# Attention and a routed expert layer on one core: result rows scattered home, batched expert numbers, latent attention a step earlier, scores in 32-row groups

## The chip, the cores and the metric

One core of one Trainium2 chip runs the whole kernel. The metric is the device time of one execution in microseconds (us), median of several runs. Everything is fp32 unless said otherwise.

## What is computed

The input x has 4 x 1024 tokens of 256 channels, 4096 tokens in 32 blocks of 128. The reference adds two branches of the layer to x; cut to what matters here:

```python
# branch 1, attention: local attention of 16 heads of 16 channels over the 128 tokens before,
# latent attention of 4 heads over means of 16 tokens, mixed by a sigmoid gate, then out_w
scores = einsum('bhnqd,bhnkd->bhnqk', qb, kb) * scale        # 32 blocks, 16 heads
attn = softmax(where(allowed, scores, NEG)); out = einsum('bhnqk,bhnkd->bhnqd', attn, vb)
lattn = softmax(einsum('bhsd,bhld->bhsl', rq, rk) * lscale)   # latent
mixed = gate * local + (1 - gate) * remote
# branch 2, experts: 64 experts (256 -> 128 -> 256), each token goes to 8 of them
tidx, tw = _gate(x, gate_w, gate_bias)
for e in experts: acc += w_dense[:, e] * ((silu(x @ wg) * (x @ wu)) @ wdn)
# and one shared expert of the same form
```

## The kernel before, in words

The five engines run hand-written streams, with semaphores between them; there is no planner. The stages follow one another in time.

**Setup** (to about 113 us): normalise x, route every token, give each of its 8 copies a slot in a table that is sorted by expert and padded to tiles of 128 rows (`slot8`, `slot_idx`), and write for each tile the number of its expert (`expert_row`, `pair_row`).

**First attention half**, `attention(0)`, blocks 0 to 15. Each engine has a `body` of eight steps `s`, one for each of eight pairs of heads. TensorE (PE): `scores(i, p)` (L833, two matmuls of 128 rows of q against 192 keys for a pair, in one of two PSUM banks `psS`), `turn_probs` (L847, transposes of the probabilities of two steps before), `values` (L859 to L861) and, spread over the steps, the projections, the shared expert and the latent attention: `latent_scores` in step 4 (L867), `latent_turn` and `latent_values` both in step 7 (L873, L879), `latent_out_turn` in step 0 of the next block (L885). The q operand `qz` is q multiplied by `own_head`, a mask of 8 columns, so that each head's 128-row column block is zero but for its own 16 rows: `keep_q` (L1480) writes 1024 values a partition, twice a block. VectorE (DVE): `mask_pair` (L1535 to L1537: mask, row maximum), `mix_sums`, `mix`, `latent_max` in step 5. ScalarE (ACT): `exps` (L1126), `keep_prT` (L1134), `latent_exp` in step 6, `keep_lprT` in step 7. Meanwhile GpSimd (POOL) scatters the normalised tokens into `slot_rows` with 256 indirect DMAs (L599), paced by waits on TensorE's progress.

**Experts**: 160 pairs of tiles. SyncE (SP) loads a pair (`load_pair`, L433, `xs`), TensorE transposes it (L944), runs gate and up (L960), and down (L969); ScalarE copies the two experts' weights from a ring of eight to `wt` (`keep_weights`, L1231 to L1236: for each tile it reads the expert's number from `expert_row` with `value_load`, L1233), applies silu (L1226) and copies the transposed tokens (`keep_tiles`, L1220); VectorE multiplies (L1614), copies the result out (`keep_y`, L1621), and for the first 128 pairs computes two routing weights (L1439). SP stores the pair to `slot_outs` (L437). POOL loads the next experts' weights into the ring (L567 to L569). The order on ScalarE in one step for pair u is `keep_weights(u+1)`, `silu(u)`, `keep_tiles(u+1)`; gate and up of pair u+1 waits for all of its copies.

**Second attention half**, `attention(HALF)`, blocks 16 to 31, with the same bodies. POOL gathers the 8 result rows of each token from `slot_outs` (256 indirect DMAs, L658, paced by TensorE's progress), and VectorE adds them, weighted, to `x_all` (`combine`, L1588). SP stores finished blocks.

## Time and profile before

| what | us |
|---|---|
| runs, median of 3 | 1552.17 (1544.11 to 1554.71) |
| the profiled execution, by its own clock | 1566.45 |
| span of its trace, first to last instruction | 1564.9 |

The profiled execution is 14.3 us (0.9%) above the median. A profile's rows are times of that one execution. An engine's "busy" is the union of its instructions; "idle before" is what lay ahead of a group's instructions, with what ended it; names ending in q are an engine's sequencer, which reads registers, waits on semaphores and issues DMAs. PE is TensorE's matmuls, PEld its weight loads.

### The profile page before, as it was taken

What the parts mean: (1) busy time and instruction counts of PE and PEld (TensorE: products, weight loads), DVE (VectorE), ACT (ScalarE), POOL (GpSimd) and SP (SyncE); (2) the same over time, 40 slices, a digit from 0 to 9 for tenths busy, and PEclk for the clock granted to TensorE, in tenths of its full rate; (3) what the DMA queues carried; (4) which work ended last, traced back from release to release, by engine and by line L of the source; (5) the groups of instructions that cost most, each with busy time, mean ns of one, the idle gap of its engine ahead of it and who ended that gap; (6) DMA issues with size and microseconds to landing.
All of it is one profiled execution on the core that took longest, in us unless ns stands there. A gap on an engine that the chain in (4) does not pass through costs nothing.

```text
span 1564.9 us, 38388 instructions
## 1 busy us (share of the span) xinstructions
PE 1349.8 (86%) x9265; PEld 1227.1 (78%) x9267; DVE 847.4 (54%) x3412; ACT 912.1 (58%) x2383; POOL 721.9 (46%) x868
## 2 busy tenths in 40 slices
PE   3946878789889889999999999999779798887986
PEld 3936777678788779898889898989678687776876
DVE  6763444444445434444444444433456777667777
ACT  2314556565555566666666666666445565555654
POOL 7525666666666602223222223100566666666662
PEclk9767989988988989999999999999988989899988
DMA  7134443342222216767777767655233223232331
GB/s 224 48 152 168 138 151 134 127 158 84 91 87 91 87 45 193 214 211 222 220 214 213 220 203 223 201 161 158 85 88 86 86 80 91 80 87 84 89 87 50
DMA packets 151276, 212.47 MB, mean 136 GB/s; under 512 B 20929, under 2 KB 126146, under 8 KB 150210
## 3 DMA queue, kind: packets, MB, share of 16 engines
q1 hardware_dynamic: 117442, 114.41, 23.5%
q0 software_dynamic: 33792, 97.56, 19.7%
q8 instruction: 19, 0.31, 0.1%
q14 instruction: 23, 0.19, 0.0%
HBM read 111.24 MB, written 100.66 MB: 135 GB/s over the span
## 4 chain that ended last, share of the span: by engine, by line
PE 76%; issue 7%; DVE 6%; another core or an unknown queue 5%; ACT 3%; SPq 2%; DVEq 0%; DMA 0%; ACTq 0%
PE psS L960 19%; PE psS L833 10%; PE psT L847 5%; PE psT L944 5%; PE psO L969 4%; PE psM L969 4%; PE psQ L780 3%; PE psV L820 2%; PE psV L791 2%; PE psT L861 2%; PE psQ L801 2%; PE psT L860 2%; PE psT L859 1%; PE psO L861 1%
## 5 line engine op out<-in xcount | busy, mean ns | idle before, releaser
L658 POOL DMA_INDIRECT shared_mem<-slot_outs,idx_st x256 | 275.3, 1075 | 153.2 <-issue 79.2
L960 PEld LDWEIGHTS psS<-sm,wt 128*128 128x128 f32 x2560 | 299.5, 193 | 40.7 <-ACT sm L1220 37.4
L599 POOL DMA_INDIRECT slot_rows<-x_out_st,idx_st x256 | 259.2, 1013 | 156.4 <-issue 58.4
L960 PE MATMUL psS<-sm,wt 128*128 128x128 f32 x2560 | 325.8, 281 | 3.3 <-ACT sm L1220 1.3
L833 PE MATMUL psS<-kT,qz 128*128 128x192 f32 x1024 | 248.0, 367 | 22.6 <-issue 11.9
L1235 ACT COPY wt<-shared_mem 128x512 f32 x320 | 197.9, 618 | 101.7 <-issue 99.3
L1134 ACT COPY prT<-psT 128x384 f32<-128x384 f32 x256 | 121.9, 476 | 222.5 <-remote 144.3
L1126 ACT ACTIVATE pr<-sm,nmax 128x192 f32<-128x192 f32 x512 | 205.1, 449 | 35.9 <-issue 17.1
L847 PE MATMUL psT<-ident,pr 128*128 128x128 f32 x768 | 141.3, 297 | 71.1 <-ACT prT L1134 56.5
L833 PEld LDWEIGHTS psS<-kT,qz 128*128 128x128 f32 x1024 | 181.3, 209 | 23.8 <-issue 19.3
L567 POOL DMA_DIRECT2D shared_mem<-in_L_ffn_We_gate x56 | 39.4, 704 | 334.4 <-PE psM L969 181.7
L1537 DVE CUSTOM_DVE_ANT_0 sm<-psS,pr 128x192 f32<-128x192 f32 x512 | 162.1, 354 | 51.9 <-issue 49.6
L847 PEld LDWEIGHTS psT<-ident,pr 128*128 128x128 f32 x768 | 100.4, 153 | 107.4 <-issue 99.9
L1614 DVE TENSOR_TENSOR prT<-psS,prT 128x256 f32<-128x256 f32 x160 | 68.0, 425 | 204.1 <-ACT prT L1226 204.1
L1588 DVE SCALAR_TENSOR_TENSOR x_all<-shared_mem,w,x_all (+1 forms) x256 | 123.9, 484 | 0.8
L1535 DVE MEMSET met<- 1x1 f32 x256 | 15.1, 59 | 198.8 <-PE psS L833 139.9
L1220 ACT COPY sm<-psT 128x512 f32<-128x512 f32 x160 | 93.7, 586 | 15.6 <-PE psT L944 9.3
L944 PE MATMUL psT<-ident,pr 128*128 128x128 f32 x640 | 97.5, 276 | 3.9 <-issue 2.3
L1226 ACT ACTIVATE prT<-psS 128x256 f32<-128x256 f32 x160 | 61.3, 383 | 54.2 <-PE psS L960 53.5
L1480 DVE TENSOR_TENSOR qz<-qT,own_head 128x1024 f32<-128x1024 f32 x64 | 78.3, 1223 | 10.9 <-ACT qT L1060 10.1
L969 PE MATMUL psO<-shared_mem,prT 128*128 x320 | 82.5, 381 | 0.2 <-DVE prT L1614 0.2
L969 PE MATMUL psM<-shared_mem,prT 128*128 x320 | 82.4, 380 | 0.0
(266 smaller groups left out, 2465.6 us busy)
## 6 DMA issues: line engine op xcount, KB each, us to landing
pr<-slot_rows SPq DMA_DIRECT2D x160, 256.0 KB, 3.1
slot_outs<-sm SPq DMA_DIRECT2D x160, 256.0 KB, 2.4
slot_rows<-wt SPq DMA_DIRECT2D x16, 512.0 KB
shared_mem<-in_L_ffn_We_gate POOLq DMA_DIRECT2D x56, 128.0 KB, 3.6
shared_mem<-in_L_ffn_We_up POOLq DMA_DIRECT2D x56, 128.0 KB, 3.8
shared_mem<-in_L_ffn_We_down POOLq DMA_DIRECT2D x56, 128.0 KB, 3.8
x_all<-in_L_attn_x SPq DMA_DIRECT2D x4, 1024.0 KB, 9.7
xn_tiles<-sm SPq DMA_DIRECT2D x32, 128.0 KB, 1.7
```

The lines of the kernel that those rows point to most:

```text
L599: pool.indirect_dma_start(slot_rows, bass.IndirectOffsetOnAxis(ap=idx_st[:, j, k:k + 1], axis=0), x_out_st[:, j % 2, :], None).then_inc(sc ...
L658: pool.indirect_dma_start(rows_in[:, j, k, :], None, slot_outs, bass.IndirectOffsetOnAxis(ap=idx_st[:, j, k:k + 1], axis=0)).then_inc(rows ...
L833: last = mm(psS[:, p % 2, u * WIN:(u + 1) * WIN], qz[:, c, u, heads, :].rearrange("p h t -> p (h t)"), kT[:, c, u * UQ:u * UQ + WIN], star ...
L847: last = nc.tensor.transpose(psT[:, 0, a * P:(a + 1) * P], flat[:, a * P:(a + 1) * P], ident[:])
L944: last = nc.tensor.transpose(psT[:, j % 2, (a * DC + c) * P:(a * DC + c + 1) * P], xs[:, j, a, c * P:(c + 1) * P], ident[:])
L960: last = mm(psS[:, j % 2, (2 * a + n) * P:(2 * a + n + 1) * P], wt[j % 2][:, a, c, n * F:(n + 1) * F], xsT[:, j % 2, a, c, :], start=(c == ...
L969: last = mm((psM, psO)[j % 2][:, a * D:(a + 1) * D], hT[:, j % 2, a, :], ring_d[:, e % RING, :], start=True, stop=True)
L1126: nc.scalar.activation(pr[:, p % 4, par, :], sm[:, p % 4, par, :], ACT.Exp, bias=nmax[:, p % 4, par:par + 1], scale=-1.0).then_inc(probs, 1)
L1134: nc.scalar.copy(prT[:, p % 2].rearrange("p a t -> p (a t)"), psT[:, 0, 0:3 * P]).then_inc(prT_ready, 1)
L1235: last = nc.scalar.copy(wt[j % 2][:, a, :, :], ring_gu[:, e % RING, :, :])
L1537: v.tensor_tensor_reduce(sm[:, p % 4, u, :], psS[:, p % 2, u * WIN:(u + 1) * WIN], mask[:, u * WIN:(u + 1) * WIN], -1.0, -FLOOR, ALU.add, ...
L1588: ins = v.scalar_tensor_tensor(x_all[:, t, :], row, w8[:, t, k:k + 1], x_all[:, t, :], ALU.mult, ALU.add)
```

## The change

- **Rows home.** A row of `slot_rows` grows from 256 to 272 words: the token's 8 slot numbers and the (negative, shifted) number of its first home row follow it. In the expert stage VectorE works out from them, for each row of a pair, which of the token's 8 places it is (`keep_meta`, five small instructions and self-waits), and POOL writes the pair's result rows to their home in `home_rows` with two indirect DMAs (`send_home`); padding rows go to spare rows. In the second half SP loads the 8 rows of a block's tokens with one plain DMA of 1 MB; POOL has nothing to do there. The expert weights' loads move from POOL to SP, the pair loads from SP to ScalarE, and the result buffers go from two to four. The stage's first pair loads wait on ScalarE for what SP waited for.
- **Expert numbers.** ScalarE reads `pair_row` (both numbers in one word) for four pairs at once, ahead of each group of four steps.
- **Latent attention.** Scores in step 3, maximum in 4, exponential in 5, transposes and their copy in 6, values in 7.
- **Scores.** `qz` is kept for two heads a 32-row group (mask `own_half`, 256 values a partition), and `scores` runs on even steps only, for two pairs at once: matmuls of 32 rows, the two pairs' in turn, in neighbouring row groups and different banks. VectorE masks both pairs in that step.

```diff
-XS, YS = 4, 2
+XS, YS = 4, 4
+ROW = 272
+META = K + 1
+HOME = T * K + 2 * YS * P
...
+            def send_home(j, u):
+                pool.wait_ge(y_kept, u + 1)
+                pool.sem_inc(blocks_begun, 1)
+                for a in range(2):
+                    pool.indirect_dma_start(home_rows, bass.IndirectOffsetOnAxis(ap=row_idx[:, j, a:a + 1], axis=0),
+                                            ys[j][:, a, :], None).then_inc(y_out[j], 16)
+
+            with pool.Fori(0, PAIRS // YS) as g:
+                for j in range(YS):
+                    send_home(j, g * YS + j)
...
+            def load_rows(j, t):
+                sp.dma_start(rows_in[:, j, :, :], home[t]).then_inc(rows_ready[j], 16)
...
-                    pe.wait_ge(masked, 2 * (n - 1))
-                heads = slice(p % PPC * 2, p % PPC * 2 + 2)
+                    pe.wait_ge(masked, 2 * n)
                 for u in range(2):
-                    last = mm(psS[:, p % 2, u * WIN:(u + 1) * WIN], qz[:, c, u, heads, :].rearrange("p h t -> p (h t)"),
-                              kT[:, c, u * UQ:u * UQ + WIN], start=True, stop=True)
-                last.then_inc(s_ready, 1)
+                    for m in (p, p + 1):
+                        r = slice(m % PPC * 2 * HD, (m % PPC + 1) * 2 * HD)
+                        last = mm(psS[:, m % 2, u * WIN:(u + 1) * WIN], qz[r, c, u, :, :].rearrange("p h t -> p (h t)"),
+                                  kT[r, c, u * UQ:u * UQ + WIN], start=True, stop=True)
+                        if u == 1:
+                            last.then_inc(s_ready, 1)
...
-                    if live:
+                    if live and s % 2 == 0:
                         scores(i, s, nth)
...
+                    if s == 6 and live:
+                        latent_turn(i)
                     if s == 7 and live:
-                        latent_turn(i)
+                        latent_values(i)
...
-                    if s == 4 and live:
+                    if s == 3 and live:
                         latent_scores(i, nth)
...
+            def experts_of(u):
+                word = act.value_load(pair_row[0:1, bass.ds(u, 1)], min_val=0, max_val=E * E - 1)
+                return word % E, word // E
+
-            def keep_weights(j, u, first):
+            def keep_weights(j, u, experts, first):
                 if not first:
                     act.wait_ge(gu_ready, u - 1)
-                for a in range(2):
-                    e = act.value_load(expert_row[0:1, bass.ds(2 * u + a, 1)], min_val=0, max_val=E - 1)
+                for a, e in enumerate(experts):
                     act.wait_ge(experts_ready, e + 1)
...
+            def load_pair(j, u):
+                act.dma_start(xs[j], slot_pairs[u]).then_inc(xs_in[j], 16)
+
...
+                if ahead and nth > 0:
+                    act.wait_ge(row_meta, u)
+                    load_pair((j + XS - 1) % XS, u + XS - 1)
...
                 with act.Fori(1, PAIRS // XS - 1) as g:
+                    named = [experts_of(g * XS + j + 1) for j in range(XS)]
                     for j in range(XS):
-                        step(j, g, MANY, False)
+                        step(j, g, MANY, False, named)
...
-                v.tensor_tensor(qz[:, c, :, :, :], bcast(qT[:, c, :].rearrange("p (u t) -> p u t", u=2), HPC, 2),
-                                bcast(bcast(own_head[:], UQ, 2), 2, 1), ALU.mult).then_inc(q_kept, 1)
+                v.tensor_tensor(qz[:, c, :, :, :], bcast(qT[:, c, :].rearrange("p (u t) -> p u t", u=2), 2, 2),
+                                bcast(bcast(own_half[:], UQ, 2), 2, 1), ALU.mult).then_inc(q_kept, 1)
...
+            def keep_meta(j, u, turn):
...
+                for a in range(2):
+                    last = v.scalar_tensor_tensor(nth_parts[:, a, :], xs[j][:, a, D:D + K], own_slot[:, j % 2, a:a + 1], nth_slot[:],
+                                                  ALU.is_equal, ALU.mult, accum_out=row_nth[:, a:a + 1])
+                last.then_inc(row_steps, 1)
+                v.tensor_scalar(own_slot[:, (j + 1) % 2, :], own_slot[:, j % 2, :], 2.0 * P, None, ALU.add)
+                dve.wait_ge(row_steps, 2 * u + 1)
+                v.tensor_tensor(nth_parts[:, :, 0], xs[j][:, :, D + K], row_nth[:], ALU.add).then_inc(row_steps, 1)
+                dve.wait_ge(row_steps, 2 * u + 2)
+                v.scalar_tensor_tensor(row_idx[:, j, :], nth_parts[:, :, 0], float(HOME), row_at[:, j, :], ALU.add, ALU.min).then_inc(row_meta, 1)
```

Also: the clearing of unused slots is cut into 32 DMAs instead of 16, each block staged for the scatter takes one more DMA of 9 words a row, and POOL prepares some 15 small constants in the setup.

## Rows read from the trace of the kernel before

**Rows 1.** Windows: the three stages. Time, busy time by engine, TensorE clock, DMA.
```profile
core 0: us, PE busy (x) PEld busy (x) DVE busy (x) ACT busy (x) POOL busy (x), PEclk, DMA share, GB/s
113.70:560.00 446.30, 369.85 (x2391) 340.67 (x2392) 209.38 (x981) 256.19 (x813) 269.47 (x288) 0.89 0.34 120
600.00:1098.00 498.00, 493.02 (x3691) 446.72 (x3690) 223.53 (x816) 337.26 (x613) 107.49 (x165) 1.00 0.67 204
1105.00:1552.00 447.00, 377.55 (x2456) 342.55 (x2456) 307.82 (x1243) 264.63 (x840) 281.62 (x287) 0.90 0.29 84
```

**Rows 2.** The chain that ended last, by engine and by line, whole span.
```profile
PE 76%; issue 7%; DVE 6%; another core or an unknown queue 5%; ACT 3%; SPq 2%; DVEq 0%; DMA 0%; ACTq 0%
PE psS L960 19%; PE psS L833 10%; PE psT L847 5%; PE psT L944 5%; PE psO L969 4%; PE psM L969 4%; PE psQ L780 3%; PE psV L820 2%; PE psV L791 2%; PE psT L861 2%; PE psQ L801 2%; PE psT L860 2%; PE psT L859 1%; PE psO L861 1%
```

**Rows 3.** Timeline of TensorE in a block of the second half: one scores group.
```profile
1528.19 0.90 PE L833 MATMUL psS<-kT,qz 128*128 128x192 f32 x4
1528.92 0.49 PE L847 MATMUL psT<-ident,pr 128*128 128x128 f32 x3
```

**Rows 4.** Groups of instructions, attention: line, engine, tiles, count, busy, mean ns, idle before.
```profile
L833 PE MATMUL psS<-kT,qz 128*128 128x192 f32 x1024 | 248.0, 367 | 22.6 <-issue 11.9 <-DVE qz L1480 9.6
L833 PEld LDWEIGHTS psS<-kT,qz 128*128 128x128 f32 x1024 | 181.3, 209 | 23.8 <-issue 19.3 <-DVE qz L1480 2.0
L879 PE MATMUL psM<-rv,lprT 128*128 (+1 forms) x128 | 24.9, 327 | 20.0 <-ACT lprT L1144 15.1 <-issue 4.8
L885 PE MATMUL psM<-ident,lat 128*128 128x128 f32 x32 | 12.3, 383 | 25.2 <-issue 20.7 <-DVE lat L1515 4.3
L847 PE MATMUL psT<-ident,pr 128*128 128x128 f32 x768 | 141.3, 297 | 71.1 <-ACT prT L1134 56.5 <-issue 13.6
L1480 DVE TENSOR_TENSOR qz<-qT,own_head 128x1024 f32<-128x1024 f32 x64 | 78.3, 1223 | 10.9 <-ACT qT L1060 10.1 <-issue 0.4
L1467 DVE TENSOR_TENSOR dif<-small,remote_z 128x256 f32<-128x256 f32 x32 | 13.4, 420 | 0.0
```

**Rows 5.** Groups of POOL: the gathers and the scatters.
```profile
L658 POOL DMA_INDIRECT shared_mem<-slot_outs,idx_st x256 | 275.3, 1075 | 153.2 <-issue 79.2 <-remote 33.7 <-PE psO L861 20.5
L599 POOL DMA_INDIRECT slot_rows<-x_out_st,idx_st x256 | 259.2, 1013 | 156.4 <-issue 58.4 <-remote 33.5 <-PE psO L861 24.5
```

**Rows 6.** Timeline of ScalarE in the expert stage.
```profile
613.12 0.58 ACT L1220 COPY sm<-psT 128x512 f32<-128x512 f32 x1
613.96 0.62 ACT L1235 COPY wt<-shared_mem 128x512 f32 x1 [0.26 <-issue]
614.80 0.62 ACT L1235 COPY wt<-shared_mem 128x512 f32 x1 [0.22 <-issue]
615.84 0.38 ACT L1226 ACTIVATE prT<-psS 128x256 f32<-128x256 f32 x1 [0.42 <-PE psS L960]
...
619.44 0.58 ACT L1220 COPY sm<-psT 128x512 f32<-128x512 f32 x1
620.60 0.62 ACT L1235 COPY wt<-shared_mem 128x512 f32 x1 [0.57 <-issue]
```

**Rows 7.** Sequencers in the expert stage: ScalarE's lookups, TensorE's, SP's loads.
```profile
L1233 ACTq FUSED_REGOPS  x613: 57/152/157, 590.7 to 1089.6; - x154
L1233 ACTq TENSOR_LOAD <-expert_row x309: 271/278/987, 590.4 to 1089.3; - x155
L1233 ACTq SEQ_ASSERT  x309: 18/18/18, 590.9 to 1089.8; - x155
...
L949 PEldq TENSOR_LOAD <-pair_row x2: 307/310/314, 607.3 to 608.0; - x2
...
L433 SPq DMA_DIRECT2D pr<-slot_rows x154: 377/378/848, 592.8 to 1088.6; - x154
DMA to landing us min/median/max: 2.6/3.1/4.6
```

**Rows 8.** Groups of VectorE and ScalarE, expert stage.
```profile
L1439 DVE SCALAR_TENSOR_TENSOR small<-shared_mem,slot 128x64 f32 x254 | 61.2, 279 | 0.0
L1621 DVE COPY sm<-psO 128x512 f32<-128x512 f32 x77 | 53.3, 692 | 43.5 <-PE psO L969 43.5
L1614 DVE TENSOR_TENSOR prT<-psS,prT 128x256 f32<-128x256 f32 x154 | 65.4, 425 | 188.3 <-ACT prT L1226 188.3
L1515 DVE TENSOR_TENSOR lat<-psM,lrec 128x64 f32<-128x64 f32 x32 | 7.2, 225 | 1.3 <-issue 0.2
```

More of the change, by code:

```diff
@@ new lines, in announce @@
+            def announce(j, g):
+                sp.wait_ge(weights_in[j], 48 * (g + 1))
+                sp.sem_inc(experts_ready, 1)
+            for j in range(2):
+                load_expert(j, RING + j)
+            with sp.Fori(1, (E - RING) // 2) as g:
+                for j in range(2):
+                    announce(j, g - 1)
+                    load_expert(j, RING + 2 * g + j)
+            for j in range(2):
+                announce(j, (E - RING) // 2 - 1)
+            sp.wait_ge(pairs_done, PAIRS + 1)
@@ new lines, in _ @@
+            for j in range(ROWS):
+                load_rows(j, j)
+            for j in range(ROWS):
+                announce_rows(j, 0)
+            with sp.Fori(1, NB // ROWS) as g:
+                for j in range(ROWS):
+                    sp.wait_ge(combined, (g - 1) * ROWS + j + 1)
+                    load_rows(j, g * ROWS + j)
+                    store_block((g - 1) * ROWS + j)
+                    announce_rows(j, g)
+            for j in range(ROWS):
+                store_block(NB - ROWS + j)
@@ L1261, in _ @@
             act.wait_ge(cleared, 16 * (E // ZROWS))
+            for j in range(2):
+                act.wait_ge(scattered[j], 16 * K * (NB // 2))
             experts()
@@ L1625, in step @@
                 make_h(j, u, nth < 2)
+                keep_meta(j, u, g)
                 if nth > 0:
-                    keep_y((j - 1) % XS, u - 1, 2 * g + (j + 1) // YS - 1, nth <= 2)
+                    keep_y((j - 1) % XS, u - 1, g if j > 0 else g - 1)
             def experts():
```

222 lines of the change are left out of this document (95 added, 127 removed).

## Prediction, made before the changed kernel ran

> **What bounds the kernel now.** I read the windows first, stage by stage, since an average over the span would mix three different limits [rows 1]. In the expert stage TensorE is busy 493.0 of 498.0 us at full clock: nothing but TensorE counts there, 160 pairs take some 3.16 us each, and no other engine may come between two pairs. The two attention halves take 446 and 447 us for about 15.7 blocks each, some 28.3 us a block, with TensorE busy 83% and 84% at a granted clock of 0.89 and 0.90; the rest is waiting. Setup and seams make up what is left. The chain of waits says the same from the other side [rows 2]: 76% TensorE, with scores 10% of 1564.9, 156 us. The groups then tell what TensorE waits for in attention [rows 4], and ScalarE's timeline how little room it has in the expert stage [rows 6].
>
> **Scores in row groups.** A pair's scores, four passes, hold TensorE from 1528.19 to 1528.92, 0.73 us, 0.18 a pass at full clock [rows 3]; 256 pairs are 187 us at that rate, 156 on the chain. Now two pairs go together, eight passes in the order g g h h g g h h over two row groups. If a pass can run beside a neighbour in the other group, but not beside one in its own, eight slots become five: 0.91 instead of 1.46 us, 0.55 less for each of 128 double pairs, 70 us. Against this, each double pair stands between full-height matmuls, so the array changes its shape twice; what a change costs no row shows. Today's weight loads run under the matmul before (181 us busy beside 248, only 23.8 idle ahead [rows 4]); without that cover one load, 0.209 on average, is bare. I take 0.15 for each of 256 changes, 38 us. Net -32. Bounds: -93 if the passes halve and a change is free, +38 if nothing overlaps and only the changes are paid.
>
> The Trainium skill ("TensorEngine Tiling (Array Packing)", Key Properties) says that changing the tiling mode, and not merely the tile, drains TensorE, and this speaks against placing the groups singly among full-height work. By its silence on a price the sum can't be made; with a drain of one pass, 0.18, at all 256 changes it would be 46 instead of 38 us. No row of this kernel shows such a change. The Trainium skill ("TensorE: Matmul & The Clock Gate", Measured speedup vs the span model) gives 3.07 times for four tiles of 32 rows; by an estimate from that page, two tiles would save about half of the 187 us, the same as the lower bound, and no row here shows it.
>
> **Latent attention a step earlier.** TensorE idles 20.0 us before the latent values, since their transposes stand just ahead and ScalarE must copy between, and 25.2 us before the turn of the result [rows 4]. A step of other work now lies between each. Of these 45 us I take 30; the rest ends on "issue", which need not be this. Bounds -45 and 0: if steps 4 and 5 of VectorE are fuller, someone else waits the little that is left.
>
> **keep_q.** 64 instructions of 1.22 us become about 0.42 each, the price of a 256-wide one [rows 4]: 51 us less on VectorE. TensorE waits on it only 9.6 us [rows 4], and VectorE is busy 47% of the first half and 69% of the second [rows 1], so it is mostly cover. I take -10; bounds -51 and 0.
>
> **Order of the scores.** The even pair's distances stay as they are; the odd pair's scores come a step earlier, so its transposes find their probabilities ready. TensorE idles 71.1 us before the transposes [rows 4]. Half of the pairs gain: -20, bounds -57 and +10 (both banks are now waited for together).
>
> **Second half without gathers.** 256 gathers, 275 us of POOL [rows 5], were paced so as to wait for TensorE, never the reverse; DMA was at 0.29 [rows 1]. VectorE's 8 additions a block stay. -5; bounds -30 (VectorE waits less for a late row) and +15 (a 1 MB load at once beside the stores).
>
> **Expert stage, ScalarE.** This is the term that costs. Sequencer and engine go in lock step here: a copy starts when the sequencer has gone through the lookup before it. After the tile copy starts (613.12) the first weight copy starts 0.84 later, the second again 0.84 later, silu, waiting for gate and up, at 2.72, after only 0.42 of idling [rows 6]. One lookup is a load of 0.278, register work of 0.06 and 0.15, an assertion of 0.018 and the gaps between, 0.60 in all [rows 7]. Now the sequencer, after a tile copy has started, does: the wait and the issue of the pair load, 0.378 on SP [rows 7], with its registers 0.55; at a group's head the loop's branch, 0.3 (1.16 from tile to weight copy there, against 0.84 [rows 6]); four lookups in a row, 2.40; addresses, 0.2. That is 3.45 until the first weight copy, then 0.65 and 0.62, and silu at 4.72 instead of 2.72: 2.0 us late. Silu of pair u+1 stands ahead of the tile copy of pair u+2, for which gate and up waits, and TensorE has no slack to give back, so each group of four pairs is 2.0 us longer: 38 loop heads and the shorter last one, 77 us. The three other pairs of a group lose nothing: 0.55 + 0.2 until the first copy, no lookup, 2.05 till the end of the second, before 2.72. Bounds: 0 if the four lookups overlap in the sequencer, of which TensorE's two in a row (0.31 each, started 0.7 apart [rows 7]) show no sign; +88 if nothing at all is hidden.
>
> **Expert stage, the rest.** VectorE has for each pair 0.43, 0.69 and two routing weights of 0.36 less an overlap, about 1.6 [rows 8]; keep_meta adds five small instructions, 0.2 to 0.28 each by the nearest ones [rows 8], with waits about 1.5. 3.1 of 3.16: hidden, the more so under the longer groups, but with nothing left; bounds 0 and +30 (0.2 on 128 pairs). POOL has two scatters, 2.6 to 2.8 us with gaps by the 1.013 and 1.075 of the halves [rows 5]: hidden. DMA moves the same rows at 0.67 share [rows 1]: 6% more on loads, hidden.
>
> **Seams.** The first pair loads start after ScalarE has finished attention, and four lookups stand ahead of the second pair: +3. The last rows go home by POOL, and q waits for them: +3. Bounds +2 and +12. Setup constants and the longer scatter rows lie beside VectorE's and TensorE's work: 0, at most +5.
>
> **Sum.** -32 - 30 - 10 - 20 - 5 + 77 + 0 + 6 = -14, against the profiled execution's 1566.45; the same difference on the median of 1552.17 gives 1538.
>
> **Rivals.**
> *The lookups are cheap.* If the four reads overlap, or their time falls under other waits, the 77 becomes 0 to 15 and everything else stands: -91 to -76, and with VectorE's part about 1470. For it: an edit that only cuts the count of lookups from 8 to 4 a group and leaves their total shorter. Against it: rows 6 and 7. Chance 0.27.
> *Slower: row groups without overlap.* If passes in neighbouring groups go one after another and each change of shape is paid, scores are +38 instead of -32 and the expert stage still loses 77: +56, 1608. It decides from the point at which a double pair takes more than 1.46 us. For it: no row here shows a 32-row pass. With half of that effect the kernel is at 1573. Chance 0.30.
> *VectorE becomes the bound of the expert stage.* keep_meta of over 1.6 us makes every pair late, whatever ScalarE does: +30 beside the cheap lookups, about 1500 in all, or hidden beside the dear ones. Chance 0.08.
> My forecast has 0.35.
>
> **How the numbers follow.** Time 1538, own range 1505 to 1570. For 8 in 10 the range reaches from 1455 to 1605. A difference under 1% can't be told from none in this kernel's runs. Faster by over 1% (below 1536.6): 0.27 and 0.07 from the first and third rivals, 0.17 of the forecast, 0.51. Within 1% (to 1567.7), which is about what a measurement of this kernel can tell from no change: 0.14 of the forecast, 0.05 of the second rival's upper part, 0.01: 0.20. Slower: 0.29.
>
> **What would show it.** Right: the expert stage at 580 to 600 us with TensorE near 87%, ScalarE's chain interrupted by 2 us once in four pairs, blocks of 25 us in attention, scores groups of about 1.2 us for two pairs, no idling before the latent values. Wrong: pairs still 3.16 us apart throughout (the lookups); scores groups of 1.5 us or more (no overlap); pairs evenly 3.4 us apart (VectorE); blocks that stay at 28 us although scores are shorter (then the bound in attention was not TensorE).

## The result, and the profile after

The changed kernel takes 1615.14 us (median of 3 runs, 1611.31 to 1615.46) against 1552.17: a ratio of 1.041, 95% interval 1.035 to 1.048. It is slower by 63 us; 1538 was forecast, with 1570 as the end of the narrow range and 1605 of the wide one. The profiled execution took 1615.46 us with a span of 1613.7, 48.8 us longer than the span of before; that is less than 63 because the profiled execution of before lay 14.3 us above its median.

For what follows one plain fact about the runs is needed: the kernel before itself was met at two levels, 1355 us beside e1 to e4 and e13 to e16, and 1552 to 1564 us in the first measurement and beside all other runs, so every ratio below is between kernels that ran side by side on one chip, and "the 1355 level" and "the 1560 level" name the two.

The windows of the three stages after the change, in the columns of [rows 1]:

```profile
106.00:560.00 454.00, 362.01 (x2397) 310.92 (x2397) 180.44 (x980) 252.15 (x811) 255.88 (x289) 0.83 0.36 128
590.00:1235.00 645.00, 536.96 (x3792) 479.34 (x3790) 320.43 (x1931) 319.61 (x631) 300.15 (x314) 0.97 0.55 165
1243.00:1600.00 357.00, 327.67 (x2448) 282.24 (x2448) 281.68 (x1241) 260.17 (x838) 1.66 (x2) 0.96 0.31 106
```

Three different things happened. The first half is where it was, with TensorE waiting more and at a lower granted clock (0.83, was 0.89). The expert stage, almost pure TensorE before and 517 us from its first to its last gate-and-up matmul, takes 650, with the engine busy 83% of the window above. The second half is 90 us shorter, and POOL has next to nothing to do in it (1.66 us). Laid end to end between the same marks of the two traces (VectorE's copy of the first and of the last block's mask in each half, first gate-and-up matmul of the first and of the last pair; the last column is after minus before):

| stretch | before | after | difference |
|---|---|---|---|
| start to the first mask | 113.7 | 105.9 | -7.8 |
| first half, 15 blocks | 432.3 | 436.0 | +3.7 |
| seam into the experts | 33.4 | 42.8 | +9.4 |
| experts | 516.9 | 650.3 | +133.4 |
| seam out | 8.5 | 7.8 | -0.7 |
| second half, 15 blocks | 421.5 | 330.5 | -91.0 |
| last mask to the end | 38.6 | 40.4 | +1.8 |

The first row is no gain of the change: e7 and e18, one and the same kernel, reach their first mask at 115.7 and 109.4 us.

The groups of the page (columns as in [rows 4]), whole span:

```profile
L956 PE MATMUL psS<-sm,wt 128*128 128x128 f32 x2560 | 341.9, 289 | 106.6 <-ACT sm L1216 88.9
L828 PE MATMUL psS<-kT,qz 32*128 32x192 f32 x1024 | 125.3, 362 | 12.3 <-DVE qz L1493 6.8
L843 PE MATMUL psT<-ident,pr 128*128 128x128 f32 x768 | 146.6, 303 | 48.7 <-ACT prT L1130 25.7
L666 POOL DMA_INDIRECT home_rows<-sm,row_idx x160 | 153.3, 958 | 195.1 <-DVE sm L1635 156.5
```

Scores are busy 125.3 us instead of 248.0 [rows 4] at an unchanged mean of 0.36 us for one (362 and 367 ns), so neighbouring row groups do overlap. TensorE's wait before the probabilities' transposes fell from 71.1 to 48.7 us. In the same view without the page's cut the latent values wait

```profile
L875 PE MATMUL psM<-rv,lprT 128*128 (+1 forms) x128 | 19.0, 275 | 0.8 <-issue 0.8
L881 PE MATMUL psM<-ident,lat 128*128 128x128 f32 x32 | 11.7, 365 | 14.7 <-DVE lat L1528 9.0 <-issue 5.7
```

0.8 us instead of 20.0, and the turn of the result 14.7 instead of 25.2. Every wait that the attention part aimed at became smaller, and the first half did not get shorter. In the expert stage gate and up now wait 106.6 us, 88.9 of them for ScalarE's copy of the turned rows. ScalarE's timeline at the head of a group of four pairs (to be read beside [rows 6]):

```profile
798.56 0.59 ACT L1216 COPY sm<-psT 128x512 f32<-128x512 f32 x1
798.72 0.38 ACTq L1238 DMA_DIRECT2D pr<-slot_rows  x1
802.64 1.14 ACT L1234 COPY wt<-shared_mem 128x512 f32 x2 [3.49 <-issue]
803.24 0.39 ACTq L1238 DMA_DIRECT2D more_mem<-slot_rows  x1
803.68 0.37 ACT L1222 ACTIVATE prT<-psS 128x256 f32<-128x256 f32 x1
803.96 0.57 ACT L1216 COPY sm<-psT 128x512 f32<-128x512 f32 x1
```

From the tile copy's start to the first weight copy's are 4.08 us at this head, and the engine idles 3.49 of them on "issue": its sequencer goes through a pair load, the branch and four lookups. Over the 39 heads of this trace the median is 3.58 until the weight copy and 4.66 until silu; the prediction had 3.45 and 4.72.

### The profile page after: what moved, and what is told of

Same layout as the page of the kernel before. It is cut to its first block, busy times and chain, and to the rows that moved or that the text cites. A ratio compares the mean times of both kernels' runs of the same rounds, so it can differ in the third digit from the quotient of the medians.

```text
span 1613.7 us, 38398 instructions
## 1 busy us (share of the span) xinstructions
PE 1316.8 (82%) x9266; PEld 1151.7 (71%) x9267; DVE 891.0 (55%) x4532; ACT 876.8 (54%) x2383; POOL 630.0 (39%) x749
## 4 chain that ended last, share of the span: by engine, by line
PE 43%; DVE 15%; issue 14%; ACTq 9%; ACT 8%; another core or an unknown queue 8%; DVEq 1%; DMA 1%; SPq 0%
PE psS L956 14%; ACTq L1226 4%; PE psS L828 4%; PE psT L843 3%; DVE x_all L1602 3%; ACTq L1238 2%; PE psV L814 2%; PE psV L785 2%; PE psT L940 2%; DVE sm L1550 2%; ACT pr L1122 2%; ACT sm L1216 2%; PE psM L965 2%; PE psQ L774 2%
## 5 line engine op out<-in xcount | busy, mean ns | idle before, releaser
L956 PE MATMUL psS<-sm,wt 128*128 128x128 f32 x2560 | 341.9, 289 | 106.6 <-ACT sm L1216 88.9
L956 PEld LDWEIGHTS psS<-sm,wt 128*128 128x128 f32 x2560 | 313.6, 200 | 153.2 <-ACT sm L1216 117.2
L639 POOL DMA_INDIRECT slot_rows<-x_out_st,idx_st x256 | 248.2, 970 | 170.4 <-issue 54.5
L1234 ACT COPY wt<-shared_mem 128x512 f32 x320 | 182.7, 619 | 140.3 <-issue 71.7
L666 POOL DMA_INDIRECT home_rows<-sm,row_idx x160 | 153.3, 958 | 195.1 <-DVE sm L1635 156.5
L666 POOL DMA_INDIRECT home_rows<-more_mem,row_idx x160 | 153.6, 960 | 194.1 <-DVE more_mem L1635 144.5
L843 PE MATMUL psT<-ident,pr 128*128 128x128 f32 x768 | 146.6, 303 | 48.7 <-ACT prT L1130 25.7
L1550 DVE CUSTOM_DVE_ANT_0 sm<-psS,pr 128x192 f32<-128x192 f32 x512 | 153.6, 354 | 36.6 <-issue 29.8
L828 PE MATMUL psS<-kT,qz 32*128 32x192 f32 x1024 | 125.3, 362 | 12.3 <-DVE qz L1493 6.8
L828 PEld LDWEIGHTS psS<-kT,qz 32*128 32x128 f32 x1024 | 84.9, 193 | 36.9 <-issue 30.1
L940 PE MATMUL psT<-ident,pr 128*128 128x128 f32 x480 | 76.7, 285 | 5.0 <-issue 4.0
L774 PE MATMUL psQ<-xTs,wqk 128*128 128x128 f32 x512 | 73.4, 303 | 0.5 <-ACT xTs L1066 0.5
```

Of the source, the lines that this page charges most:

```text
L639: pool.indirect_dma_start(slot_rows, bass.IndirectOffsetOnAxis(ap=idx_st[:, j, k:k + 1], axis=0), x_out_st[:, j % 2, :], None).then_inc(sc ...
L666: pool.indirect_dma_start(home_rows, bass.IndirectOffsetOnAxis(ap=row_idx[:, j, a:a + 1], axis=0), ys[j][:, a, :], None).then_inc(y_out[j] ...
L828: last = mm(psS[:, m % 2, u * WIN:(u + 1) * WIN], qz[r, c, u, :, :].rearrange("p h t -> p (h t)"), kT[r, c, u * UQ:u * UQ + WIN], start=Tr ...
L843: last = nc.tensor.transpose(psT[:, 0, a * P:(a + 1) * P], flat[:, a * P:(a + 1) * P], ident[:])
L956: last = mm(psS[:, j % 2, (2 * a + n) * P:(2 * a + n + 1) * P], wt[j % 2][:, a, c, n * F:(n + 1) * F], xsT[:, j % 2, a, c, :], start=(c == ...
L1234: last = nc.scalar.copy(wt[j % 2][:, a, :, :], ring_gu[:, e % RING, :, :])
```

## The experiments

### First set: lookups, way home, gathers, scores

e1 puts the lookup back in front of each pair (and drops the reads at a group's head):

```diff
-                    keep_weights((j + 1) % XS, u + 1, named[j], nth == 0)
+                    keep_weights((j + 1) % XS, u + 1, experts_of(u + 1), nth == 0)
```

Expected: 

> The changed kernel with the four-pair lookups undone: one read of pair_row ahead of each pair's weight copies. Theory L (the batch of four lookups, 2.4 us in one go, is what the expert stage lost): the long gaps once in four pairs vanish, the stage falls from 645 to about 515 us, 1615 to about 1490. Theory G (GpSimd's indirect DMAs hold up TensorE's signals to the other engines, and the lookups are only one part of the loss): 77 us at most go, 1535 to 1560, and pairs of 4 to 5 us remain, scattered. Rival: a lookup in every pair is itself exposed behind the DMA issue, 0.1 to 0.4 us a pair, and only 20 to 60 us go.

e2 sends the result rows with plain DMAs, so they don't go to their own places:

```diff
-                    pool.indirect_dma_start(home_rows, bass.IndirectOffsetOnAxis(ap=row_idx[:, j, a:a + 1], axis=0),
-                                            ys[j][:, a, :], None)
+                    pool.dma_start(home_rows[bass.ds(u % 128 * (2 * P) + a * P, P), :], ys[j][:, a, :])
```

Expected: 

> The changed kernel, but GpSimd writes the result rows with two plain DMAs of the same 128 rows of 1 KB to rows in order, not to their home (the output then lacks the right expert rows). Theory G: no update of a TensorE semaphore comes late in the expert stage, as before the change; the stage loses 40 to 70 us, total 1545 to 1575. Theory L, or a theory of DMA traffic or of ScalarE's DMA issue: the stage stays at 640 to 650 us, total 1610 to 1615.

e3 is the kernel before with its gathers as plain DMAs, so the rows combined are not the right ones:

```diff
-                    pool.indirect_dma_start(rows_in[:, j, k, :], None, slot_outs,
-                                            bass.IndirectOffsetOnAxis(ap=idx_st[:, j, k:k + 1], axis=0))
+                    pool.dma_start(rows_in[:, j, k, :], slot_outs[bass.ds(i * (K * P) + k * P, P), :])
```

Expected: 

> The kernel before, with the 256 gathers of the second half made plain DMAs from GpSimd, same size, same pacing, rows in order (wrong rows are added). Theory G: the second half falls from 28.1 us a block to 23 to 25, total 1470 to 1505, and no TensorE update comes late there. Rival (the second half became shorter in the changed kernel through scores, latent attention and keep_q): it stays at 28, total 1545 to 1555.

e4 is the kernel before with the scores part alone (row groups, pairs in twos, narrow q; its lines are those of the change's diff). Expected: 

> The kernel before with the scores in 32-row groups and the narrow q alone. My prediction's terms (-32, -10, -20): 1490. Theory G: where indirect DMAs run, TensorE's own work is not what sets a block, so 1535 to 1552. If row groups do not overlap: scores groups of 1.5 us or more for two pairs and 1550 to 1590.

Measured, before at 1354.85: e1 1362.03, ratio 1.0044 [1.0030, 1.0058]; e2 1420.99, 1.0485 [1.0460, 1.0511]; e3 1353.96, 0.9993 [0.9983, 1.0003]; e4 1375.55, 1.0145 [1.0104, 1.0185]. So at this level the lookups were nearly all of the loss, the kind of the gathers' transfers did nothing (e3), and the scores part alone was a loss, as large as its expectation had put it for groups that don't overlap, though they do. The times in us that were expected of e1 to e3 can't be compared: the kernel before was 200 us faster than in its first measurement, and what its first trace had shown in both halves was gone here.

That thing is the following, in the trace of before, inside the first half (PE, DVE, ACT and POOL; columns: start, duration, engine, instruction, and in brackets the idle time before it with its releaser):

```profile
307.78 0.96 POOL L599 DMA_INDIRECT slot_rows<-x_out_st,idx_st  x1 [0.30 <-issue]
308.48 0.49 PE L847 MATMUL psT<-ident,pr 128*128 128x128 f32 x3
...
309.05 0.96 POOL L599 DMA_INDIRECT slot_rows<-x_out_st,idx_st  x1 [0.30 <-issue]
309.18 0.39 PE L861 MATMUL psO<-va,prT 128*128 128x36 f32 x2
309.40 0.90 PE L833 MATMUL psS<-kT,qz 128*128 128x192 f32 x4
310.38 0.98 POOL L599 DMA_INDIRECT slot_rows<-x_out_st,idx_st  x1 [0.17 <-issue]
312.46 0.48 ACT L1134 COPY prT<-psT 128x384 f32<-128x384 f32 x1 [3.55 <-remote]
312.52 0.06 DVE L1535 MEMSET met<- 1x1 f32 x1 [4.06 <-remote]
313.08 0.52 PE L847 MATMUL psT<-ident,pr 128*128 128x128 f32 x3 [2.79 <-ACT prT L1134]
```

The transposes ended at 308.97, the values at 309.57 and the scores at 310.30. ScalarE's copy waits on TensorE for transposes and values, VectorE's mask for scores, yet both start only at 312.5. TensorE then waits 2.79 us for the copy. "remote" is how the view names a signal that it can't put down to an instruction's end. In the semaphore events five signals of TensorE that were due between 308.0 and 310.3 all arrive within 312.33 to 312.57, about 1 us after the end of the third of GpSimd's indirect transfers in a row. Counted over the trace (late: over 0.3 us behind the modelled end of the matmul that gives the signal): 203 of 431 signals in the first half, 0 of 460 in the expert stage, 169 of 364 in the second half. Those are the stages with and without indirect transfers on GpSimd. In the changed kernel's first trace: many in the first half, 117 of 360 in the expert stage, 0 of 524 in the second half; again where the transfers are. In e3, whose first half still has such transfers, and in e4, whose halves both have them, no signal is late; both ran at the 1355 level. Two theories were therefore on the table: L, the lookups; and G, indirect transfers on GpSimd hold TensorE's signals up, in a condition that the first set of runs did not meet.

### Second set: the change itself, and its parts

e5 is the change itself. Expected: 

> The changed kernel itself, with the kernel before on one chip. The runs so far were beside a kernel before of 1355 us, with one lookup per pair at a ratio of 1.0044, and with four lookups at the head of a group of four pairs (and plain transfers home) at 1.0485. Theory L (the four lookups at once are nearly the whole of the loss): a ratio of 1.04 to 1.05, with one pair in four of the expert stage lasting 5.0 us instead of 3.16, and TensorE's signals on time. Theory G (indirect transfers home hold up TensorE's signals, as in the first trace of the change): a ratio above 1.06, since e2 had plain transfers.

e6 is e1's kernel with the scores of before (`qz` at its full size; two result buffers and one input buffer lie in `qz` during the expert stage, as there is no other room). Expected: 

> The change with one lookup per pair and with the old scores (full height, one pair per step); rows written home and latent attention one step earlier stay. Theory S (the scores in 32-row groups cost time in the second half, 22.3 to 22.8 us per block instead of 21.7): blocks of 21.0 to 21.5 us in the second half and 20.3 in the first, a ratio of 0.98 to 0.99. Rival H (loads of home rows and the plan with four buffers cost it): second-half blocks stay at 22.5 us and the first half goes back to 21, a ratio of 1.01 to 1.02.

e7 is the kernel before with

```diff
-                    if s == 4 and live:
+                    if s == 3 and live:
                         latent_scores(i, nth)
```

and the other latent steps one earlier in the same way. Expected: 

> The kernel before with latent attention one step earlier and nothing else. Theory W (TensorE waits there for the latent probabilities, and the move takes that wait away): first-half blocks of 20.3 us instead of 21.0 and second-half blocks of 21.0 instead of 21.7, a ratio of 0.983. Rival N (the wait is already covered when TensorE's signals are on time): a ratio of 0.998 to 1.002.

e8 takes the row groups without the twos:

```diff
-                  mm(psS[...], qz[:, c, u, heads, :]..., kT[:, c, u * UQ:u * UQ + WIN], ...)
+                  mm(psS[...], qz[r, c, u, :, :]..., kT[r, c, u * UQ:u * UQ + WIN], ...)
```

Expected: 

> The kernel before with the narrow q and the scores in 32-row groups, but one pair per step as before: two matmuls of the same row group, no interleaving, masks in the old order. Theory M (the 32-row groups themselves cost: the change of shape before and after them and a lower granted clock): as slow as e4 or slower, a ratio of 1.01 to 1.03. Rival O (the order in twos costs it: TensorE waits for both masks, and VectorE does two masks in a row before its other work): a ratio of 0.99 to 1.00.

Measured, before at 1564.01: e5 1643.74, ratio 1.0507 [1.0447, 1.0566]; e6 1578.67, 1.0050 [1.0009, 1.0091]; e7 1563.29, 0.9981 [0.9949, 1.0012]; e8 1659.73, 1.0591 [1.0523, 1.0659]. Latent attention alone is worth nothing that can be told here. Row groups one pair at a time cost 96 us, twice what theory M had put as its most. e5 falls between what L and what G gave it (to 1.05, from 1.06), and e6 between its two ranges. In e5 the expert stage shows in one place both of its losses (PE, ACT, POOL):

```profile
722.01 0.96 POOL L666 DMA_INDIRECT home_rows<-more_mem,row_idx  x1 [0.87 <-DVE more_mem L1635]
722.36 0.63 PE L940 MATMUL psT<-ident,pr 128*128 128x128 f32 x4 [0.17 <-issue]
...
723.24 1.14 ACT L1234 COPY wt<-shared_mem 128x512 f32 x2 [3.15 <-issue]
723.28 0.96 POOL L666 DMA_INDIRECT home_rows<-more_mem,row_idx  x1 [0.30 <-issue]
725.00 0.39 ACT L1222 ACTIVATE prT<-psS 128x256 f32<-128x256 f32 x1 [0.62 <-remote]
725.28 0.58 ACT L1216 COPY sm<-psT 128x512 f32<-128x512 f32 x1
725.91 0.82 PE L956 MATMUL psS<-sm,wt 128*128 128x128 f32 x5 [2.06 <-ACT sm L1216]
```

The 3.15 on "issue" are ScalarE's sequencer with pair load, branch and lookups. The silu behind them waits another 0.62 for a signal due at 722.2, and the tile copy for one due at 723.0; three signals of TensorE land between 724.90 and 725.02, after the second of the pair's two indirect transfers. First to last gate-and-up took 669.4 us in e5 and 621.9 in e6, which has one lookup per pair and still the transfers.

### Third set: theory G put to the test where signals are late

Expected of e9, e3's kernel: 

> The kernel of e3 again (the kernel before, its 256 gathers through index lists replaced by plain transfers of as many bytes, so that the rows combined are not the right ones), because e3 ran where the kernel before takes 1355 us and no signal of TensorE was late. Theory G (indirect transfers on GpSimd's queue are what delays TensorE's semaphore updates, where they are late): if the kernel before takes some 1560 us here, second-half blocks fall from about 27.5 to 21.7 us, no update there is late, the first half stays at 29 us, and the ratio is near 0.94; if it takes 1355 us, the ratio is 1.00 again. Rival (lateness comes with the stage, not with the kind of transfer): a ratio of 0.99 to 1.00 on either.

Expected of e10, e1's kernel with e2's plain transfers: 

> The change with one lookup per pair and with plain transfers home (rows not at their right places). Theory G: where the kernel before takes some 1560 us, the expert stage has pairs of 3.16 us with no late signal and lasts 520 us as in e1, and the ratio is near 0.96; where it takes 1355 us, the ratio is that of e1, 1.00. Rival: where signals are late, they stay late in the expert stage, and the ratio stays at 1.005 or above.

Expected of e11, e4's kernel: 

> The kernel of e4 again (the kernel before with the scores in 32-row groups, two pairs interleaved, and the narrow q), beside e12 on the same chip. Theory M (32-row groups themselves cost time): a ratio of 1.01 to 1.03, and clearly above that of e12. Rival O (the order in twos costs it): the same ratio as e12.

Expected of e12, which keeps full-height scores and full q:

```diff
-                    if live:
+                    if live and s % 2 == 0:
                         scores(i, s, nth)
```

with both pairs' matmuls one after the other, and both masks in that step: 

> The kernel before with its full-height scores and its full q, but issued for two pairs at once at every second step, and the masks in twos. Theory M: a ratio of 0.99 to 1.00, since the shapes are those of before. Rival O: a ratio of 1.01 to 1.03, the same as e11.

Measured, before at 1562.37: e9 1459.17, ratio 0.9341 [0.9294, 0.9389]; e10 1496.95, 0.9585 [0.9537, 0.9634]; e11 1592.13, 1.0186 [1.0133, 1.0240]; e12 1566.38, 1.0018 [0.9991, 1.0044].

e9 shows G for the gathers. Only the kind of transfer in the second half differs from before. Its windows of the first and the second half:

```profile
115.00:540.00 425.00, 346.00 (x2244) 318.78 (x2242) 195.08 (x906) 239.19 (x761) 264.21 (x285) 0.88 0.34 119
1110.00:1419.00 309.00, 300.46 (x2226) 283.93 (x2224) 274.49 (x1124) 231.30 (x755) 134.63 (x267) 1.00 0.37 113
```

The first half, with its indirect scatters, is as slow as ever: TensorE busy 81% at 0.88. The second, same code but for the transfers, has it busy 97% at full clock: blocks of 21.7 us, exactly as at the 1355 level, instead of 28.1. ScalarE's waits in the second half say how, first in the trace of before, then in e9 (total us, times, longest):

```profile
ACT prT L1134 <- remote: 68.0, 17, 10.4
ACT prT L1134 <- PE psT L847: 21.2, 18, 1.4
```

```profile
ACT prT L1133 <- PE psT L846: 26.4, 33, 1.4
```

No signal is late in e9's second half (0 of 534 after 1100 us). e10 points the same way for the change: with plain transfers home its expert stage lasts 520.1 us from first to last gate-and-up, against 621.9 in e6 with indirect ones, and none of 460 signals is late. e6 is no exact pair to it: it has the scores and buffer places of before, it ran on another chip, and its profiled execution (1585.62 us) is 7 us above its median, so the second price below is the rougher one. What the late signals of a stage cost is thus seen twice, 101 us beside 256 gathers (421.5 us of second half before, 320.9 in e9) and some 102 beside 320 sends. GpSimd is busy 0.96 us with each send and over 1 with each gather; how the signals and these transfers meet inside the chip the traces don't show. Nor are the transfers enough by themselves: at the 1355 level the same ones run with every signal on time, and the condition that has to be added stays unknown. It is not one particular chip: e1 to e4 and e9 to e12 ran on the same one.

e11 and e12 settle the scores: the order in twos costs nothing that can be told, the shape, with the narrow q that goes with it, does. The windows 115:543 of e12 and 115:557 of e11, and 115:573 of e8:

```profile
115.00:543.00 428.00, 351.07 (x2279) 325.39 (x2279) 196.98 (x923) 239.05 (x770) 263.74 (x285) 0.90 0.34 118
```

```profile
115.00:557.00 442.00, 359.34 (x2258) 308.75 (x2259) 170.26 (x917) 239.45 (x769) 251.13 (x285) 0.79 0.33 114
```

```profile
115.00:573.00 458.00, 422.89 (x2276) 358.82 (x2274) 175.92 (x925) 243.81 (x773) 252.64 (x286) 0.79 0.33 114
```

With about as many matmuls in each, TensorE's granted clock is 0.90 with full-height scores and 0.79 with those of 32 rows. e8 is the telling one: nothing overlaps there, the engine is busy 92% of the window, more than in e12 (82%), and it is granted less. It also prices the shape itself, at full clock:

```profile
1269.37 0.91 PE L836 MATMUL psS<-kT,qz 32*128 32x192 f32 x4
1270.21 0.55 PE L850 MATMUL psT<-ident,pr 128*128 128x128 f32 x3
```

One pair's four passes, all in one row group, take 0.84 us from start to start, where they took 0.73 in full height [rows 3]: 0.11 us for both changes of shape and whatever the passes themselves may take longer, 28 of the 96 us over 256 pairs if all ran at full clock. Why the granted clock is lower with these passes the traces don't show.

In e4 the low clock can be seen in a block of the second half at the 1355 level (windows of 2 us):

```profile
1158.20:1160.20 2.00, 2.00 (x20) 1.66 (x19) 1.75 (x6) 0.57 (x3) 1.39 (x3) 1.00 0.23 78
1160.20:1162.20 2.00, 1.69 (x15) 1.60 (x16) 2.00 (x13) 1.56 (x5) 1.51 (x2) 1.00 0.45 131
1162.20:1164.20 2.00, 1.48 (x13) 1.23 (x12) 1.88 (x5) 1.78 (x6) 1.57 (x2) 0.97 0.32 86
1164.20:1166.20 2.00, 1.97 (x10) 1.36 (x10) 1.56 (x6) 1.42 (x6) 1.39 (x3) 0.50 0.34 111
1166.20:1168.20 2.00, 2.00 (x8) 1.73 (x8) 1.74 (x12) 1.20 (x4) 1.73 (x3) 0.50 0.54 156
```

TensorE idles 0.31 and 0.52 us in the two windows ahead of the drop, waiting for ScalarE's copies of the local and of the latent probabilities; then 6.8 us go by at 1.2 GHz instead of 2.4, and so in every block from 1110 us to 1320. The timeline around there has the scores at full clock and after the drop:

```profile
1159.27 0.92 PE L837 MATMUL psS<-kT,qz 32*128 32x192 f32 x8
1160.12 0.55 PE L852 MATMUL psT<-ident,pr 128*128 128x128 f32 x3
...
1164.41 1.65 PE L837 MATMUL psS<-kT,qz 32*128 32x192 f32 x8
```

At full clock eight passes go from 1159.27 to 1160.12, 0.85 us, where two pairs took 1.46 before [rows 3]; that is as long as e8's four, so the second row group costs nothing more. Added up per block by the distance from one matmul's start to the next, scores fell from 5.7 to 3.4 us in the first half of e4 against e3; 1.5 of those 2.3 came back at the transposes and the values, 0.1 elsewhere, and the block shrank by 0.8 (21.0 to 20.2). In the second half 5.7 became 4.1, and the block grew by 2.2 (21.6 to 23.8): 2.4 at the transposes and the values, 1.3 at the output projection and the shared expert's last matmuls, which run at half clock.

### Fourth set: how the loss divides

This set met the 1355 level (before at 1355.05).

e13 is e1's kernel. Expected: 

> The change with one lookup per pair (e1's kernel again). Where the kernel before takes some 1560 us, theory D (the loss has two near-equal parts, late signals in the expert stage and the four lookups, each worth 50 to 110 us): ratio 1.00 to 1.02, the expert stage some 600 us instead of 650 to 670. Theory L (the lookups are nearly all of it): a ratio below 0.98. Rival (the lookups hide behind the late signals there): a ratio of 1.04 or more. Where the kernel before takes 1355 us: 1.0044 as in e1.

e14 is e2's. Expected: 

> The change with plain transfers home and the four lookups (e2's kernel again; the rows do not go to their right places). Where the kernel before takes some 1560 us, theory D: ratio 0.99 to 1.01, with pairs of 3.16 us and one in four of 5.0 us, as e10 at 0.9585 plus some 57 us for the lookups (0.995). Rival (late signals matter little in the expert stage): 1.03 or more. Where the kernel before takes 1355 us: 1.0485 as in e2.

e15 is the change with the scores of before, laid out as in e6. Expected: 

> The change with the old scores (full height, one pair per step), the four lookups and the indirect transfers home kept. Theory M (32-row groups are a loss, since the granted clock falls): faster than e16 by 0.5 to 2 per cent. Rival (they gain inside the change, where latent attention is earlier and the second half has no late signals): slower than e16 by as much.

e16 is the change. Expected: 

> The change itself again. Where the kernel before takes some 1560 us: a ratio of 1.04 to 1.05, as in its first measurement and in e5. Where the kernel before takes 1355 us: theory L, 1.045 to 1.05, the same as e2, since indirect and plain transfers home differ by nothing there; rival, 1.06 or more, if indirect transfers home cost there too, which e1 at 1.0044 speaks against.

Measured: e13 1366.14, ratio 1.0067 [1.0042, 1.0093]; e14 1425.12, 1.0517 [1.0484, 1.0550]; e15 1429.53, 1.0555 [1.0524, 1.0585]; e16 1424.58, 1.0506 [1.0482, 1.0530]. With signals on time the change loses 69.5 us: 58.4 are the four lookups (e16 against e13), nothing is the kind of transfer home (e14 against e16), and the scores part is even worth 5 us inside the change (e15 against e16). Alone it had cost 20.7 (e4). The clock has a part in that: in the second half e4 is granted 0.89 (1000 to 1330 us), but e16 0.97 (1060 to 1380), where the latent values no longer wait; that this wait is the reason is not shown, since e16 differs from e4 in more. Windows of 570 and 510 us inside the expert stages of e16 and e13:

```profile
470.00:1040.00 570.00, 508.96 (x3756) 457.57 (x3757) 316.53 (x1923) 317.82 (x626) 297.96 (x310) 0.99 0.61 186
```

```profile
470.00:980.00 510.00, 503.81 (x3763) 456.63 (x3763) 318.78 (x1917) 325.79 (x627) 298.84 (x311) 1.00 0.68 208
```

From first to last gate-and-up e16 takes 580.2 us and e13 520.1; e16's pairs are 5.0, 3.2, 3.16 and 3.16 us apart, in turn. Its ScalarE at a head:

```profile
801.68 0.59 ACT L1216 COPY sm<-psT 128x512 f32<-128x512 f32 x1
...
805.33 1.14 ACT L1234 COPY wt<-shared_mem 128x512 f32 x2 [3.06 <-SPq L457]
...
806.37 0.37 ACT L1222 ACTIVATE prT<-psS 128x256 f32<-128x256 f32 x1
```

3.65 us pass until the weight copy and 4.69 until silu, against 2.73 until silu in a pair without lookups. e13 is within 3 us of before in that stage although VectorE has 62% of it (45% before [rows 1]): `keep_meta` is hidden. But e13 gains nothing overall either, and e16's trace shows where its shorter first half (19.6 us a block) goes:

```profile
433.42 1.06 PE L815 MATMUL psV<-wsd,hsT 128*128 128x256 f32 x2
...
434.54 0.96 POOL L639 DMA_INDIRECT slot_rows<-x_out_st,idx_st  x1 [0.30 <-issue]
435.80 0.96 POOL L639 DMA_INDIRECT slot_rows<-x_out_st,idx_st  x1 [0.30 <-issue]
...
457.42 0.96 POOL L639 DMA_INDIRECT slot_rows<-x_out_st,idx_st  x1 [0.30 <-issue]
460.03 1.48 ACTq L1238 DMA_DIRECT2D pr<-slot_rows  x3
...
463.05 1.12 PE L940 MATMUL psT<-ident,pr 128*128 128x128 f32 x4 [28.58 <-DMA pr<-slot_rows]
```

Attention is over at 434.5, but the scatters, 1.27 us apart, go on until 458.4, and the experts need all rows. TensorE stands still for 28.6 us, where in e3 it was 18.0. The 19.6 us gained in the first half (311.2 to 291.6 from first to last mask) shrink to 3.5 at the first gate-and-up (468.3 in e3, 464.8 in e16). The second half is no gain either: 330.5 us in e16 against 320.9 in e3. With the scores of before (e15) it is 325.5 and the seam ahead of it 4.3 us longer, so what is left there lies with the other parts of the change; which of them was not tested.

### Fifth set: does any part pay?

e17 puts two parts into the kernel before: latent attention earlier, and the grouped scores in the first half only:

```diff
-                    if live and s % 2 == 0:
+                    if live and (s % 2 == 0 or not grouped[0]):
                         scores(i, s, nth)
```

Expected: 

> The kernel before with latent attention one step earlier in both halves, and the scores in interleaved 32-row groups with the narrow q in the first half only; rows are gathered and loaded as before, lookups one per pair. Where the kernel before takes 1355 us: first-half blocks of 19.6 us instead of 21.0 and second-half blocks of 21.7 as before or a little less, a ratio of 0.98 to 0.987. Rival (latent attention earlier hurts or helps the second half by itself): second-half blocks away from 21.7 by over 0.4 us, a ratio outside of 0.975 to 0.99. Where the kernel before takes some 1560 us: 1.00 to 1.01, since e11 lost in both halves there and e7 gained nothing.

e18 is e7's kernel. Expected: 

> The kernel before with latent attention one step earlier (e7's kernel again). Where the kernel before takes 1355 us, theory W (TensorE's wait there goes): first-half blocks of 20.3 to 20.7 us instead of 21.0, a ratio of 0.985 to 0.995; rival N (the time of a full-height block is TensorE's own work, so nothing is left to take away): 0.998 to 1.002. Where it takes some 1560 us: 0.998 as in e7.

Measured, before at 1563.76: e17 1569.83, ratio 1.0048 [1.0019, 1.0077]; e18 1557.05, 0.9965 [0.9933, 0.9997]. e18 is 0.35% faster, e7 said 0.2%: at most a few us. No version that computes the same beat the kernel before by 1%. Neither was met at the 1355 level, for which both were meant. There e16's seam lets one expect that the scatters would take most of e17's gain; and e15, which has latent attention earlier with the scores of before, is 2 us shorter than e3 in its first half.

## Why the prediction was wrong

Two steps failed. The one that decides the sign, at both levels, is common to "Scores", "Latent attention", "keep_q" and "Order of the scores": that busy time and waits taken from TensorE are taken from the block. They are -92 us in the sum. In the first traces they came out as +14, and at the 1355 level, without any late signal, the first half and the second of e16 differ from e3's by -19.6 and +9.6 us, and the seam takes 14.0 back. So the forecast of a gain fails there too: the change loses 69.5 us, although the lookups cost less than forecast.

**The other step that failed is "Expert stage, the rest", in its sentence on POOL**: two scatters per pair, 2.6 to 2.8 us of 3.16, "hidden", priced at nothing. Their time is hidden; their effect on TensorE's signals isn't. At the 1560 level it costs some 102 us (e6 against e10 from first to last gate-and-up), and it was neither in the sum nor a rival. The trace of before held the hint: TensorE busy 99% in the one stage without indirect transfers and 83 or 84% in the two with them [rows 1], "another core or an unknown queue" in the chain of a program on one core [rows 2], and "remote" behind the idle time of L658 and L599 [rows 5]. The prediction took these as waiting in attention in general.

**"Second half without gathers"** is the same mistake with the other sign: -5, bounds -30 and +15, measured -101 by e9. That the two nearly cancel is luck: the hold-up moved from one stage to the other at the 1560 level, and the kind of transfer is worth nothing either way at the 1355 level (e14 against e16, e3).

**The lookups, +77.** The mechanism was right, the size a third too high: 58.4 us at the 1355 level, 47.5 at the other (e5 against e6 in the expert stage, two executions whose late signals differ too). ScalarE's chain came almost as forecast, silu 4.71 us after the tile copy (median of e16's 39 heads) for 4.72, and 2.73 for 2.72 in the other pairs. But eight pairs take 29.2 us in e16 and 26.0 in e13, so a group is 1.6 us longer and not 2.0. Most of the 0.4 is the loop's turn: the prediction counted it as new, but the kernel before pays it too, once in eight pairs (3.8 instead of 3.16 us, 0.3 for each group of four).

**Scores, -32.** TensorE's own saving was put too low: a double pair, with both changes of shape in it, takes 0.85 us at full clock, where the prediction had 0.91 and 0.30 more. The eight slots became four and not five, and 128 double pairs would save some 78 us at that rate. The step that failed is that what TensorE saves is time saved. The part alone is +20.7 us (e4) and +29.8 (e11), because the engine then waits for ScalarE and is granted a lower clock. The Trainium skill ("TensorEngine Tiling (Array Packing)", Key Properties) says that changing the tiling mode drains TensorE. The traces leave little for it here: 0.11 us for both changes around a group, if a pass takes as long as in full height (e8), which is 14 us for 128 double pairs against the 38 of the prediction. The rival "row groups without overlap" gave 1608, near the measured time, by luck: its condition, over 1.46 us for a double pair, isn't met.

**Latent attention, -30, and the order, -20.** The latent values' wait went (20.0 to 0.8 us), those of the result's turn and of the transposes fell (25.2 to 14.7, 71.1 to 48.7), and none of it was time: -0.7 us in e7 and -6.7 in e18; the order alone +4.0 (e12), the interval of its ratio holding 1. keep_q's -10 was not measured alone.

**Seams, +6.** +8.7 in the first traces; at the 1355 level POOL's scatters decide there, a bound I had not named.

**keep_meta, 0.** Right within 3 us (e13's expert stage is 520.1 us, e3's 517.1).

The forecast of -14 becomes the +48.8 of the first traces so, if the sends cost there what they cost between e10 and e6; the 31 us left for the lookups is a remainder and no measurement: +102 for the sends; -96 since the gathers were worth 101 and not 5; +106 since the 92 us of gains in attention (scores, latent, keep_q, order) came out as +14 (first half +3.7, second -91.0 less the gathers' -101); -46 since the experts' +133.4 leaves 31 for the lookups in that trace; and -3 for setup and seams (+2.7 instead of +6).

## What to carry to other kernels

Before a wait of TensorE in the profile is priced as removable, compare its stages. Where TensorE's signals are late ("remote" as releaser in a program on one core) only in the stages in which GpSimd issues indirect transfers, try those transfers as plain ones first: here that was worth 101 us where signals were late and nothing where they were on time. What one engine's sequencer reads at the head of a group comes as one lump: four reads of 0.6 us cost at most 3 us over the whole stage one at a time and 1.6 us a group together. And work taken from TensorE is only gained if it doesn't come back as waiting or as a lower granted clock, and if no seam follows at which another engine, here POOL's scatters at 1.27 us each, sets the time.

## What the runs showed of the hardware that was not expected

- Signals of TensorE came late by up to 4.3 us in the rows above, several at once, in 203 of 431 cases beside GpSimd's indirect transfers at the 1560 level; never beside plain ones, and never at the 1355 level beside either. Why a run is at one level or the other stays open; the same kernels were met at both, and so was one chip.
- TensorE's granted clock is lower with 32-row scores than with full-height ones even when the engine is busier: 0.79 at 92% busy (e8) against 0.90 at 82% (e12), in the first half.
- Two neighbouring row groups do run beside each other: eight passes of 192 columns in two groups take 0.85 us at full clock (e4), four in one group 0.84 (e8), four in full height 0.73.
